# The selective scan of a four-layer model: sums over the states by transposing matmuls, and two of eight products dt*x*B by another route

## The reference, cut to what matters

```python
dt = jax.nn.softplus(dt + dt_bias[None, :, None])
A = -jnp.exp(A_log)
def step(h, inp):                      # one token
    x_t, dt_t, B_t, C_t = inp
    dA = jnp.exp(dt_t[..., None] * A)
    dBx = dt_t[..., None] * B_t[:, None, :] * x_t[..., None]
    h = dA * h + dBx
    y = jnp.einsum('bdn,bn->bd', h, C_t)
    return (h, y)
y = (ys + D_param[None, :, None] * xc) * jax.nn.silu(z)
return jnp.einsum('bdl,hd->blh', y, out_proj_w)
```

## Time and profile before

| | us |
|---|---|
| median of 3 runs | 5363.93 |
| lowest, highest | 5358.28, 5369.31 |
| the profiled execution | 5354.56 |
| span of its trace | 5352.8 |

### The profile page before, as it was taken

The page is one execution under the profiler, slowest core; times in us unless marked ns, Lnnn a source line. Parts: engine busy times, 40 slices in busy tenths (PEclk is TensorE's granted clock), DMA queues, the critical chain, the costliest instruction groups (busy, mean ns, idle before and its releaser), DMA issues. The chain is left out here.

```text
span 5352.8 us, 40461 instructions
## 1 busy us (share of the span) xinstructions
PE 4902.7 (92%) x14496; PEld 2349.2 (44%) x14496; DVE 3251.4 (61%) x3534; ACT 1881.3 (35%) x2677; POOL 2309.7 (43%) x1219
## 2 busy tenths in 40 slices
PE   8998989999868899968789999999999999999998
PEld 4443234467536444423333444444444344457443
DVE  1663468756457322239999999999999722103522
ACT  1554620045322111125555555555555410002100
POOL 1003420000022000019999999999999742100421
PEclk8899999999989999989999999999999999999999
DMA  2001030000010121142116436444644320000001
GB/s 75 1 1 67 32 118 24 28 17 1 9 34 1 40 68 67 50 123 53 42 40 174 133 124 179 140 133 134 181 140 124 127 82 0 24 0 27 22 16 47
DMA packets 180006, 360.84 MB, mean 67 GB/s; under 512 B 21790, under 2 KB 56734, under 8 KB 175710
## 3 DMA queue, kind: packets, MB, share of 16 engines
q1 hardware_dynamic: 171742, 330.45, 20.4%
q0 software_dynamic: 8064, 27.80, 1.4%
HBM read 300.50 MB, written 57.67 MB: 67 GB/s over the span
## 5 line engine op out<-in xcount | busy, mean ns | idle before, releaser
L2851 POOL TENSOR_TENSOR l2scan_h<-l2scan_dtx,l2scan_Bb 128x1024 f32<-128x1024 f32 x512 | 1198.2, 2358 | 30.8 <-DMA l2scan_Bb<-l_bc 15.0
L2753 PE MATMUL l2scan_yp<-l2scan_h,ident 128*128 128x512 f32 x2048 | 971.5, 608 | 115.1 <-POOL l2scan_h L2876 101.1
L2820 ACT ACTIVATE l2scan_ring<-l2scan_dt,l2scan_A 128x512 f32<-128x512 f32 x1024 | 663.9, 681 | 639.4 <-DVE l2scan_h L2932 481.0
L2753 PEld LDWEIGHTS l2scan_yp<-l2scan_h,ident 128*128 128x128 f32 x2048 | 389.3, 193 | 639.4 <-issue 481.1
L2743 PE MATMUL l2scan_low_z<-state,l2scan_Wz 128*128 128x512 f32 x1024 | 476.6, 598 | 0.3
L2876 POOL TENSOR_TENSOR l2scan_h<-l2scan_h,l2scan_Cb 128x1024 f32<-128x1024 f32 x192 | 452.1, 2355 | 8.6 <-DVE l2scan_h L2921 0.9
L2411 PE MATMUL l2in_acc<-state,l2in_W 128*128 128x512 f32 x1024 | 444.9, 595 | 10.5 <-DMA l2in_W<-l_attn_in_x 10.5
L2932 DVE TENSOR_TENSOR l2scan_h<-l2scan_ring,l2scan_Cb 128x1024 f32<-128x1024 f32 (+1 forms) x384 | 394.3, 1041 | 6.1 <-DMA l2scan_Cb<-l_bc 0.7
L2921 DVE TENSOR_TENSOR_SCAN l2scan_ring<-l2scan_ring,l2scan_carry,l2scan_h 128x512 f32<-128x512 f32 x320 | 392.7, 1273 | 0.0
L2921 DVE TENSOR_TENSOR_SCAN l2scan_ring<-l2scan_ring,l2scan_h 128x512 f32<-128x512 f32 x320 | 373.3, 1212 | 5.5 <-POOL l2scan_h L2851 5.5
L2538 PE MATMUL l2scan_oacc<-l2scan_oy,l2scan_oW 128*128 128x512 f32 x768 | 353.1, 592 | 0.0
(11 more groups left out here) (409 smaller groups left out, 7538.2 us busy)
## 6 DMA issues: line engine op xcount, KB each, us to landing
l2scan_oy<-l_y SPq DMA_DIRECT2D x192, 512.0 KB, 4.9
l2scan_Wz<-l_attn_in_z SPq DMA_DIRECT2D x64, 512.0 KB, 3.6
l2scan_oW<-l_attn_out_w SPq DMA_DIRECT2D x192, 128.0 KB, 3.3
l_xc<-l2in_xc SPq DMA_DIRECT2D x16, 1024.0 KB, 4.8
l2scan_xc<-l_xc SPq DMA_DIRECT2D x64, 256.0 KB, 5.7
l2scan_Bb<-l_bc SPq DMA_DIRECT2D x128, 128.0 KB, 6.9
l2scan_Cb<-l_bc SPq DMA_DIRECT2D x128, 128.0 KB, 7.8
l_y<-l2scan_zs SPq DMA_DIRECT2D x64, 256.0 KB, 5.5
```

The lines of the kernel that those rows point to most:

```text
L2753: last = t.matmul(yp[:, :], K.ident[:, :], h[:, st % SLOTS, j, :], start=g == 0 and j == 0, stop=g == NSG - 1 and j == SGR - 1)
L2820: a.activation(bank(st, j), dt[:, q % 2, :], ACT.Exp, scale=A[:, ct, n:n + 1]).then_inc(dA_ok, 1)
L2851: g_.tensor_tensor(h[:, st % SLOTS], dtx[:, None, :].to_broadcast([P, SGR, NT]), Bb[:, g * SGR:(g + 1) * SGR, :], ALU.mult).then_inc(dBx_o ...
```

## The change

Three things are changed together.

1. The sum over the states. `total` now issues, for each state, four 128x128 matmuls in transposing mode, one for each block of 128 tokens: the block of `h` and the identity go in, and the turned block is added into a new PSUM tile `yT`, which has tokens on the partitions. When the eight pairs of an item are in, ScalarE copies `yT` to SBUF (`keep`, at g = 1 ahead of `gate`), TensorE turns the four blocks back into `yp` (`turn_back`, at g = 2), and `finish` moves on VectorE from behind step 1 to behind step 2. `yT` takes a PSUM bank, so the ring of exponentials has four banks instead of five.
2. `MAKERS = "PPPTPPPT"`: the pairs dt*x*B of g = 3 and g = 7 are no longer made by GpSimd. Once an item TensorE turns `dtx` (`turn_dtx`, g = 6) and ScalarE copies it out (`keep_dtx`); once a chunk the rows of B are turned in the same way (`turn_rows`, `columns`). Then a pair is eight ScalarE instructions on 128x128 blocks, each scaled by one column of B (`products`, issued one step ahead), and eight transposes on TensorE into the two ring banks (`turn_products`). For these steps the exponentials go to the slot of `h`, and `Bb` holds and loads twelve rows instead of sixteen.
3. `KINDS = "YWYWYWYW"`: the product with C of step 7 goes from VectorE to GpSimd.

```diff
-KINDS = "YWYWYWYY"
+KINDS = "YWYWYWYW"
+MAKERS = "PPPTPPPT"
-    BANKS = 5
+    BANKS = 4
...
@@ TensorE
                 def total(st):
                     q, g = divmod(st, NSG)
                     wait_hC(t, st)
                     if g == 0 and q:
+                        t.wait_ge(copied, q)
+                    for j in range(SGR):
+                        for k in range(BLOCKS):
+                            last = t.matmul(yT[:, k, :], h[:, st % SLOTS, j, k * P:(k + 1) * P], K.ident[:, :], is_transpose=True,
+                                            start=g == 0 and j == 0 and k == 0, stop=g == NSG - 1 and j == SGR - 1 and k == BLOCKS - 1)
+                    last.then_inc(summed, 1)
...
+                def turn_dtx(q):
+                    t.wait_ge(dtx_ok, q + 1)
+                    if q % CT == 0:
+                        t.wait_ge(bt_ok, q // CT + 1)
+                    if q >= 2:
+                        t.wait_ge(y_ok, q - 1)
+                    elif q:
+                        t.wait_ge(dx_ok, q)
+                    for k in range(BLOCKS):
+                        last = t.transpose(yp[:, k * P:(k + 1) * P], dtx[:, k * P:(k + 1) * P], K.ident[:, :])
+                    last.then_inc(dx_ready, 1)
+
+                def turn_products(st):
+                    n = made("T", st)
+                    t.wait_ge(prod_ok, n)
+                    for j in range(SGR):
+                        wait_bank(t, st, j)
+                        for k in range(BLOCKS):
+                            last = t.transpose(bank(st, j)[:, k * P:(k + 1) * P], prod[:, n % 2, j, k, :], K.ident[:, :])
+                    last.then_inc(dBxT_ok, 1)
+
+                def turn_back(q):
+                    t.wait_ge(copied, q + 1)
+                    t.wait_ge(dx_ok, min(q + 2, ITEMS))
+                    if q:
                         t.wait_ge(y_ok, q)
-                    for j in range(SGR):
-                        last = t.matmul(yp[:, :], K.ident[:, :], h[:, st % SLOTS, j, :], start=g == 0 and j == 0, stop=g == NSG - 1 and j == SGR - 1)
-                    last.then_inc(summed, 1)
+                    for k in range(BLOCKS):
+                        last = t.transpose(yp[:, k * P:(k + 1) * P], ysb[:, k, :], K.ident[:, :])
+                    last.then_inc(turned_back, 1)
...
                 for st in range(STEPS):
                     q, g = divmod(st, NSG)
+                    if maker(st) == "T":
+                        turn_products(st)
+                    if g == 2 and q:
+                        turn_back(q - 1)
                     if g != 1 and st >= 2:
                         total(st - 2)
...
+                    if g == 6 and q + 1 < ITEMS:
+                        turn_dtx(q + 1)
...
@@ ScalarE
+                def keep(q):
+                    a.wait_ge(summed, (q + 1) * NSG)
+                    if q:
+                        a.wait_ge(turned_back, q)
+                    a.activation(ysb[:, :, :], yT[:, :, :], ACT.Copy).then_inc(copied, 1)
...
+                def keep_dtx(q):
+                    a.wait_ge(dx_ready, q + 1)
+                    if q:
+                        a.wait_ge(prod_ok, made("T", q * NSG - 1))
+                    a.activation(dtxT[:, :, :], yp[:, :].rearrange("p (k d) -> p k d", d=P), ACT.Copy).then_inc(dx_ok, 1)
+
+                def products(st):
+                    q, g = divmod(st, NSG)
+                    c, n = q // CT, made("T", st)
+                    a.wait_ge(bt_ok, c + 1)
+                    a.wait_ge(dx_ok, q + 1)
+                    if n > 2:
+                        a.wait_ge(dBxT_ok, n - 2)
+                    for j in range(SGR):
+                        for k in range(BLOCKS):
+                            s_ = g * SGR + j
+                            last = a.activation(prod[:, n % 2, j, k, :], dtxT[:, k, :], ACT.Copy, scale=BT[:, c % 2, k, s_:s_ + 1])
+                    last.then_inc(prod_ok, 1)
...
+                    if maker(st) == "T" and st >= SLOTS:
+                        a.wait_ge(summed, st - SLOTS + 1)
                     for j in range(SGR):
                         n = g * SGR + j
-                        wait_bank(a, st, j)
-                        a.activation(bank(st, j), dt[:, q % 2, :], ACT.Exp, scale=A[:, ct, n:n + 1]).then_inc(dA_ok, 1)
+                        if maker(st) == "P":
+                            wait_bank(a, st, j)
+                        a.activation(bank(st, j) if maker(st) == "P" else h[:, st % SLOTS, j, :], dt[:, q % 2, :], ACT.Exp, scale=A[:, ct, n:n + 1]).then_inc(dA_ok, 1)
                     if g == 1 and q:
+                        keep(q - 1)
                         gate(q - 1)
                     if g == 3 and q + 1 < ITEMS:
                         split(q + 1)
                     if g == 4 and q + 1 < ITEMS:
                         log1p(q + 1)
+                        if (q + 1) % CT == 0:
+                            columns((q + 1) // CT)
+                    if st + 1 < STEPS and maker(st + 1) == "T":
+                        products(st + 1)
+                    if g == 6 and q + 1 < ITEMS:
+                        keep_dtx(q + 1)
+                keep(ITEMS - 1)
                 gate(ITEMS - 1)
...
@@ GpSimd
                 def make_dBx(st):
                     q, g = divmod(st, NSG)
+                    if maker(st) == "T":
+                        return
...
@@ VectorE
-                    v.wait_ge(summed, (q + 1) * NSG)
+                    v.wait_ge(turned_back, q + 1)
...
+                        dA, dBx = (bank(st, j), hs[:, j, :]) if maker(st) == "P" else (hs[:, j, :], bank(st, j))
+                        last = v.tensor_tensor_scan(out, dA, dBx, init, ALU.mult, ALU.add)
...
-                    if g == 1 and q:
+                    if g == 2 and q:
                         finish(q - 1)
```

More of the change, by code:

```diff
@@ L2555, in l2_scan @@
     SLOTS = 6
-    BANKS = 5
+    BANKS = 4
     LEAD = 3
+    BLOCKS = NT // P
     with Stage(nc, "l2scan") as s:
-        Bb = s.sb("Bb", [P, NS, NT])
+        Bb = s.sb("Bb", [P, SGR * MAKERS.count("P"), NT])
         Cb = s.sb("Cb", [P, NS, NT])
@@ L2606, in upto, with made, rows_at @@
             return q * KINDS.count(k) + KINDS[:g].count(k)
+        def made(k, st):
+            q, g = divmod(st + 1, NSG)
+            return q * MAKERS.count(k) + MAKERS[:g].count(k)
+        def rows_at(g):
+            at = SGR * MAKERS[:g].count("P")
+            return slice(at, at + SGR)
         def carries(k, st):
@@ L2663, in rows_b @@
                 def rows_b(c, g):
+                    if maker(g) == "T":
+                        return
                     if c:
-                        e.wait_ge(dBx_ok, (c * CT - 1) * NSG + g + 1)
-                    rows(Bb[:, g * SGR:(g + 1) * SGR, :], B_AT + g * SGR, c, b_in[g])
+                        e.wait_ge(dBx_ok, made("P", (c * CT - 1) * NSG + g))
+                    rows(Bb[:, rows_at(g), :], B_AT + g * SGR, c, b_in[g])
                 def rows_c(c, g):
@@ L2750, in total, with turn_rows @@
                     if g == 0 and q:
+                        t.wait_ge(copied, q)
[4 more added lines that the diff above has]
+                    last.then_inc(summed, 1)
+                def turn_rows(c):
+                    t.wait_ge(ssm_in[c % 2], 16 * (c // 2 + 1))
+                    if c:
+                        t.wait_ge(y_ok, c * CT - 1)
+                        t.wait_ge(dx_ok, c * CT)
+                    for k in range(BLOCKS):
+                        last = t.transpose(yp[:, k * P:(k + 1) * P], ssm[:, c % 2, k * P:(k + 1) * P], K.ident[:, :])
+                    last.then_inc(bt_ready, 1)
@@ L2757, in _ @@
+                turn_dtx(0)
                 for st in range(STEPS):
                     q, g = divmod(st, NSG)
+                    if maker(st) == "T":
+                        turn_products(st)
+                    if g == 2 and q:
+                        turn_back(q - 1)
                     if g != 1 and st >= 2:
@@ L2766, in _ @@
                         dt_tile(q + 1)
+                    if g == 4 and q + 1 < ITEMS and (q + 1) % CT == 0:
+                        turn_rows((q + 1) // CT)
+                    if g == 6 and q + 1 < ITEMS:
+                        turn_dtx(q + 1)
                     if g == 5:
@@ L2807, in gate, with columns @@
                     a.preload_act_table_set(LOG_EXP)
+                def columns(c):
+                    a.wait_ge(bt_ready, c + 1)
+                    if c >= 2:
+                        a.wait_ge(prod_ok, made("T", (c - 1) * CT * NSG - 1))
+                    a.activation(BT[:, c % 2], yp[:, :].rearrange("p (k r) -> p k r", r=P)[:, :, B_AT:B_AT + NS], ACT.Copy).then_inc(bt_ok, 1)
+                def keep_dtx(q):
[11 more added lines that the diff above has]
+                    for j in range(SGR):
+                        for k in range(BLOCKS):
+                            s_ = g * SGR + j
```

(7 more changed lines are left out.)

23 lines of the change are left out of this document (19 added, 4 removed).

## The result

The changed kernel takes 5660.66 us (median of 4 runs, 5653.81 to 5667.95) against 5361.1 for the kernel before in the same session: ratio 1.0557, 95% interval [1.0538, 1.0577], some 300 us slower. The prediction had 5550 and at most 5640. The direction was right, and 110 us are missing from it.

What follows compares the result with a forecast made beforehand. VectorE and GpSimd were taken as full before, a closed ring of waits after: 31.2 us plus 0.4 hand-overs and 0.2 carry copies, 31.8 against 28.93 an item; 181 us plus start and end, 186, gave 5550, range 5450 to 5640.

Steps and rivals of the forecast that it cites:

- direction: Whole kernel: the change makes it slower, chance 0.88; faster 0.09, same 0.03.
- ring: Cycle of waits through TensorE's turn of pair 7, ScalarE, VectorE and GpSimd, one item per turn: 31.8 us an item.
- What the reader must check is that no step of the ring has slack: After `pre_dt`, VectorE's step 7 scan ends at 8.4 us, GpSimd reaches its product at 10.7, so GpSimd is last.
- Rival 3: TensorE's lower clock for sparse transposes: pair 7's turn doubles, 1.04 us an item, 66 us more, 5616; chance 0.09.
- Sums of work: Work per engine and item: VectorE 28.2 us before, 26.9 after; GpSimd 28.3 before, 26.0 after; TensorE 27 after, ScalarE 22.
- The 27 us: Item time by engine work alone, without waits: some 27 us, a gain of 115 us.
- 2.3 + 3.63 + 2.37: VectorE from `pre_dt` through step 5 to the end of step 7's scan: about 8.4 us.
- Rival 1: Ring doesn't close because pair 7 is summed before ScalarE reaches `keep`: 27.2 us an item, 5261 us; chance 0.09.
- Signs: If right: `finish` every 31 to 32.5 us, VectorE under 87% busy, its largest waits step 2 and `pre_c`, ScalarE's `keep`.
- Small terms: ScalarE's products for a step 2.28 us; `keep`, `gate` and sum to `pre_c` 0.60 + 3.21 + 8.48; VectorE's part 4.92.

Runs made afterwards that it cites:

- experiment 15: Changed kernel with step 7's products turned ahead of the second z part and unused transposes in TensorE's gaps: 5552 us, ratio 1.0361.
- Experiment 4: Changed kernel with `gate` ahead of `keep` on ScalarE at g = 1: 5467 us, ratio 1.0202.
- experiment 3: Changed kernel with TensorE's two gaps before the first z part filled by unused 128x128 transposes: 5566 us, ratio 1.0389.
- the last version: Changed kernel with `keep` and `keep_dtx` later, products of steps 3 and 7 turned earlier, three projection pieces one g later, no unused transposes: 5292 us, ratio 0.9876.

## Why the prediction was wrong, by its steps

- **Direction and ring: right.** `keep` behind the eighth pair, the eighth pair behind GpSimd's queue, that behind `pre_dt`, that behind `log1p`. Its sum, 31.6 us and 32.0 with the two carry copies, is what experiment 15 shows in settled items (31.6 and 32.0). That its whole time is 5552 for 5550 is in part luck: its mean item is 31.98 for 31.8, which over 63 items is 11 us. Experiment 4 shows that ScalarE's part is on the ring.
- **"What the reader must check is that no step of the ring has slack": this step failed.** It compared GpSimd's queue with VectorE's step 7 and passed over TensorE with the words that `turn_dtx` and `z_part` wait for dt "as before". TensorE's queue behind `pre_dt` is the first z part, pair 4, dtx, the second z part and step 7's products: at full clock 2.6 + 0.9 + 0.4 + 2.6 + 1.1 and a hand-over of 0.15, 7.7 us, and 2.45 for the scans, 10.2; GpSimd reaches its product after 10.7. The path is covered by half a us (experiment 3 shows both times), which the sum never showed. With 5.25 for the first z part and 1.23 for pair 4 the same path takes 13.2, 2.5 us late: that is GpSimd's wait of 2.51 and the 2.5 us between the settled items. The whole cost was 5661 - 5552 = 109 us.
- **Rival 3 had the clock, but in the wrong place.** It put the lower level on the turn of pair 7 (measured 1.09 us for eight, the full clock in chunk 3) and dismissed the z matmuls, because busy stretches regain the clock. They do, but only behind the 5.25 us that count; the earlier trace rows already showed six z instructions of 3.96 us not long behind a wait, and six of 2.74 a little later. The waits ahead of it come from the relief of TensorE itself: before, it waited for GpSimd's pairs 4.7, 9.6 and 5.0 us in the whole of chunks 1, 2 and 3, and in the item of the earlier trace rows it ran through this stretch without a gap.
- **Sums of work: nearly right, and without effect on the forecast.** The 27 us were a bound that the written order doesn't reach; with another order of the same work settled items of chunk 3 take 27.4 us. VectorE's terms add up to 27.8 us before and 26.6 after, not 28.2 and 26.9, and 2.3 + 3.63 + 2.37 is 8.3, not 8.4; neither is a term of the ring.
- **Rival 1 didn't happen:** `keep` waited 64 times, 167 us in all.
- **Signs.** VectorE is busy 79% of the second stretch (under 87% was forecast) and `keep` waits, but the item of 33.73 us lies above 31 to 32.5, and the largest waits of VectorE and ScalarE are at TensorE's queue behind the first z part.
- **Small terms:** 2.34 for 2.28, 12.37 for 12.3, 4.91 for 4.92.

## What to carry to other kernels

When work is moved between engines that are all full, walk every queue that the new waits pass, each with what stands ahead of the awaited instruction, and write down the slack of each path: one covered by half a microsecond is the next bound. An engine that is relieved begins to wait, and TensorE paid for it here behind the wait, in instructions that nobody changed (5.25 us for 2.59). A slower stretch costs time only where its delay isn't covered: in chunk 0 of the last version it costs next to nothing. Fix the order before filling gaps: unused work gave 94 us while the order was bad and cost 62 us once it was good.
